# Attention kernel: TensorE's order from a search over 128 partial plans, and four sets of softmax weights instead of three

## The chip, the cores and the metric

The program runs on one core of a Trainium2 chip, in one launch. The metric is the device time of that launch in microseconds (us), the median of several runs. Five engines work side by side, each through its own list of instructions in order: TensorE (PE, with PEld for its weight loads), VectorE (DVE), ScalarE (ACT), GpSimd (POOL) and SyncE (SP), which issues the DMAs here. They are held together by semaphores.

## The reference, cut to what matters

One block: attention with a latent space per head, layer norm, a mixture of eight experts with top-2 routing, layer norm. x is (4, 2048, 256), there are 16 heads, and the latent width L is 32. The change is in the attention:

```
q_for_k = q_lat @ wqk_w.T + wqk_b
att = jnp.einsum('bhql,bhkl->bhqk', q_for_k, k_lat) * L ** (-0.5)
causal = jnp.tril(jnp.ones((T, T), dtype=bool))
att = jnp.where(causal[None, None], att, -jnp.inf)
att = jax.nn.softmax(att, axis=-1)
y_lat = jnp.einsum('bhqk,bhkl->bhql', att, v_lat)
```

## The kernel before, in words

The stages run one after the other: projections (`project_heads`), attention (`attend`), mixing and routing (`mix_and_route`), experts, final norm.

Attention is cut into 16 slots (batch by group of HG = 4 heads), each with NC = 4 chunks of CH = 512 queries, so 64 chunks. TensorE has four kinds of work there:

- A **unit** (`max_unit`, L855): one matmul of 128 queries against up to 512 keys, only to find each query's maximum. VectorE reads the bank and reduces it: L996 below the diagonal, L1000 with the causal edge added on it. 2560 units, four banks (MAXB).
- A **score** (`score`, L867): one matmul of 128 keys against up to 512 queries, with the negative maximum carried in two extra rows of q. ScalarE takes its exponential into `probs` (L941). 2560 scores, three banks (SCOREB). Four scores, one a head, make a key step.
- A **weigh** (`weigh`, L883): the four heads' weights of one key step times v, four matmuls into four groups of 32 partitions of one bank, `acc`. 640 weighs. In the trace each matmul has two records, so a full step is eight. They use the array in a narrow form (128 x 32), the others the whole array; the code calls this "tiled".
- A **turn** (`turn_sums`, L894): at the end of a chunk ScalarE copies `acc` (L931), TensorE transposes it, VectorE divides (L1027, L1031).

`probs` holds PROBS = 3 key steps: the exponentials of step k wait until weigh k - 3 is done. On the diagonal GpSimd masks the weights before the weigh (L980). The maxima of a chunk are combined, split and transposed on VectorE (L1006 to L1022) behind the chunk's last unit. SyncE then puts them into q's extra rows with eight small DMAs (L784, `put_shift`), and only then may the chunk's first score start. SyncE's list also holds the loads of q, k and v for later chunks (`load`) and the stores of y (`store_y`).

The order of these four kinds of work is fixed when the kernel is built, by the class `Order`. It plays the stage through with a clock of its own (`now`) and durations for each engine, and at each step takes the work with the lowest price. A weigh that follows a weigh is taken first up to BURST = 2; a first weigh is dearer when fewer than GATHER = 2 are ready. The lists that come out (`units_before_score`, `scores_before_weighing` and the like) set TensorE's order and, through the same lists, where ScalarE reads `acc`, where VectorE divides, and where SyncE puts rows and stores y. These engines' own work keeps its sequence.

Of the kernel before, what the change touches and what calls it, by code (L numbers as in the profile page):

```python
# [10 lines left out]

# [14 lines left out]
P = 128  # L26
# [3 lines left out]
HG = P // L  # L30
G = H // HG
CH = 512
NC = T // CH
TT = CH // P
# [487 lines left out]
BURST = 2  # L522
GATHER = 2
EVEN = 0.1
JOIN = 0.1
MAXB, SCOREB = 4, 3
PROBS = 3
# [4 lines left out]
def chunk_of(s, c):  # L532
    return s * NC + c
# [20 lines left out]

class Order:


    MODE, DRAIN = 0.112, 0.17

    def __init__(self):  # L560
        self.units_before_score = [0] * NS
        self.scores_before_weighing = [0] * NK
        self.units_before_weighing = [0] * NK
        self.scores_before_turn = [0] * CHUNKS
        self.units_before_turn = [0] * CHUNKS
        self.weighed_before_turn = [0] * CHUNKS
        self.now, self.tiled, self.burst = 0.0, False, 0
        self.u = self.h = self.w = self.turned = 0
        self.vector = self.scalar = self.pool = self.queue = 0.0
        self.reduced, self.exped, self.weighed = [0.0] * NU, [0.0] * NS, [0.0] * NK  # L570
        self.masked, self.read, self.divided = {}, {}, {}
        self.rows, self.parts_due = {}, []
        while self.h < NS or self.w < NK or self.turned < CHUNKS:
            self.step()

    def starts(self):

        free, tiled = self.now + self.MODE * self.tiled, self.now + self.MODE * (not self.tiled)
        at = {}
        u, h, w = self.u, self.h, self.w  # L580
        if u < NU and chunk_of(*MU[u][:2]) - chunk_of(*KS[min(h, NS - 1) // HG][:2]) <= QBUF - 2:
            at["unit"] = max(free, self.reduced[u - MAXB] if u >= MAXB else 0.0)
        if h < NS and h // HG - PROBS < w:
            s, c, kt = KS[h // HG]
            first = h % HG == 0 and kt == 0
            if not first or chunk_of(s, c) in self.rows:
                at["score"] = max(free, self.exped[h - SCOREB] if h >= SCOREB else 0.0,
                                  self.rows[chunk_of(s, c)] if first else 0.0)
        if w < NK and HG * (w + 1) <= h:
            s, c, kt = KS[w]  # L590
            n = chunk_of(s, c)
            if kt or n == 0 or n - 1 in self.divided:
                at["weigh"] = max(tiled, self.exped[HG * w + HG - 1], self.masked.get(w, 0.0),
                                  self.divided[n - 1] if kt == 0 and n else 0.0)
        if self.turned in self.read:
            at["turn"] = max(free, self.read[self.turned])
        return at

    def step(self):
        at = self.starts()  # L600
        backlog = {"unit": max(self.vector - self.now, 0.0), "score": max(self.scalar - self.now, 0.0)}
        if self.tiled and "weigh" in at and self.burst < BURST and at["weigh"] - self.now <= JOIN:
            pick = "weigh"
        elif not self.tiled and "turn" in at and at["turn"] <= self.now + 0.05:
            pick = "turn"
        else:
            price = {}
            for kind, start in at.items():
                price[kind] = start - self.now
                if kind in backlog:  # L610
                    price[kind] += EVEN * backlog[kind]
# [9 lines left out]
        start = at[pick]  # L621
        if pick == "weigh":
            self.weigh(start)
        elif pick == "unit":
            self.unit(start)
        elif pick == "score":
            self.score(start)
        else:
            self.turn(start)

    def weigh(self, start):
        k = self.w
        self.scores_before_weighing[k], self.units_before_weighing[k] = self.h, self.u
        self.burst = self.burst + 1 if self.tiled else 1
        self.tiled = True
        self.now = start + (CH - first_query(k)) / 600 + 0.03
        self.weighed[k] = self.now + self.DRAIN
        n = chunk_of(*KS[k][:2])
        if k + 1 == LAST_STEP[n]:
            self.scalar = max(self.scalar, self.weighed[k]) + 0.49  # L640
            self.read[n] = self.scalar + 0.16
        self.w += 1
# [1367 lines left out]
```

## Time and profile before

| | us |
|---|---|
| median of 3 runs | 2953.5 (2951.43 to 2960.58) |
| the profiled execution | 2953.24 |
| its span | 2951.5 |

| engine | busy us | share of the span |
|---|---|---|
| PE | 2811.8 | 95% |
| PEld | 1915.6 | 65% |
| DVE | 2124.7 | 72% |
| ACT | 1828.5 | 62% |
| POOL | 803.5 | 27% |

The first unit of attention starts at 367.0 us and the last division ends near 2147, so attention takes 1780 of the 2951.5 us. A matmul's record includes the time in which its columns are still in the array, so records of neighbouring matmuls overlap, and "busy" hides short waits. The distance from one start to the next tells more.

### The profile page before, as it was taken

The numbers are of one execution on the slowest core, as the hardware profiler recorded it, in microseconds if no ns is written. First come the engines' busy times: TensorE is split into PE (matmuls) and PEld (weight loads), VectorE is DVE, ScalarE is ACT, GpSimd is POOL, SyncE is SP. The second block draws the span as 40 slices with busy tenths as digits, with TensorE's granted clock in tenths as the row PEclk, the third lists the DMA queues.
The fourth block names the chain that finished last, engine by engine and source line by source line (L and its number), as shares of the span: only waits on it lengthen the run. The fifth ranks groups of instructions, "written<-read, shape, count | busy, mean of one in ns | idle before, by whom it ended". The sixth has DMA issues, their size and how long they took to land. (4 is left out here: it accounts for less than half of the span.)

```text
span 2951.5 us, 48579 instructions
## 1 busy us (share of the span) xinstructions
PE 2811.8 (95%) x16538; PEld 1915.6 (65%) x16538; DVE 2124.7 (72%) x5590; ACT 1828.5 (62%) x3673; POOL 803.5 (27%) x785
## 2 busy tenths in 40 slices
PE   8999989999999999999999999999979996999991
PEld 7888755555555655555555555555457774899991
DVE  7888788888888888888888888888334443545444
ACT  5666535766666676666666676666745453655554
POOL 7888620110110110111111011011025554122332
PEclk9999978999999999999999999999989998999995
DMA  7787852413332432432431432331053320434326
GB/s 227 265 286 265 290 130 55 106 43 88 91 91 75 95 83 70 109 80 59 108 96 43 94 82 63 88 82 32 5 166 121 108 83 24 120 74 105 78 25 236
DMA packets 259529, 320.32 MB, mean 109 GB/s; under 512 B 70563, under 2 KB 157644, under 8 KB 258001
## 3 DMA queue, kind: packets, MB, share of 16 engines
q1 hardware_dynamic: 241616, 294.02, 35.3%
q0 software_dynamic: 17664, 23.19, 3.9%
q8 instruction: 132, 2.16, 0.3%
q14 instruction: 117, 0.95, 0.1%
HBM read 182.69 MB, written 143.95 MB: 111 GB/s over the span
## 5 line engine op out<-in xcount | busy, mean ns | idle before, releaser
L941 ACT ACTIVATE att_probs<-att_score_bank 128x512 f32<-128x512 f32 (+3 forms) x2560 | 1159.0, 549 | 590.2 <-PE att_score_bank L867 582.3
L996 DVE TENSOR_REDUCE att_partial_max<-att_max_bank 128x1 f32<-128x512 f32 x1536 | 1004.9, 687 | 119.1 <-PE att_max_bank L855 113.6
L855 PE MATMUL att_max_bank<-att_k_st,att_q_st 96*128 96x512 f32 (+3 forms) x1792 | 642.2, 382 | 7.9 <-DVE att_partial_max L996 6.8
L867 PE MATMUL att_score_bank<-att_q_st,att_k_st 98*128 98x512 f32 (+3 forms) x1792 | 641.4, 384 | 2.4 <-ACT att_probs L941 2.3
L1000 DVE CUSTOM_DVE_ANT_0 att_edge_sum<-att_max_bank,first_edge 128x128 f32<-128x128 f32 (+3 forms) x1024 | 481.9, 483 | 150.9 <-PE att_max_bank L855 150.5
L883 PE MATMUL att_acc_bank<-att_probs,att_v_st 128*32 128x512 f32 (+3 forms) x5120 | 545.5, 539 | 1.4 <-POOL att_probs L980 0.9
L980 POOL TENSOR_SCALAR_AFFINE_SELECT att_probs<-att_probs 128x512 f32<-128x512 f32 x256 | 162.8, 636 | 1314.9 <-ACT att_probs L941 1314.9
L867 PEld LDWEIGHTS att_score_bank<-att_q_st,att_k_st 98*128 98x128 f32 x1792 | 334.2, 188 | 188.8 <-ACT att_probs L941 107.2
L855 PEld LDWEIGHTS att_max_bank<-att_k_st,att_q_st 96*128 96x128 f32 x1792 | 344.0, 193 | 149.3 <-DVE att_partial_max L996 74.7
L883 PEld LDWEIGHTS att_acc_bank<-att_probs,att_v_st 128*32 128x32 f32 x5120 | 132.1, 109 | 246.1 <-issue 135.8
L241 POOL TENSOR_TENSOR proj_op_low<-proj_turned,proj_op_high 128x512 fp32r<-128x512 f32 x192 | 244.2, 1295 | 47.0 <-ACT proj_op_high L401 44.8
L1733 ACT ACTIVATE exp_hid_high<-exp_hid_bank,exp_b 128x512 fp32r<-128x512 f32 x128 | 88.3, 690 | 160.8 <-PE exp_hid_bank L1680 150.8
L1647 POOL DMA_INDIRECT z_rows<-exp_eo,exp_row_ids x64 | 108.3, 1692 | 288.9 <-DVE exp_eo L1792 258.9
L855 PE MATMUL att_max_bank<-first_k,att_q_st 96*128 96x512 f32 (+3 forms) x432 | 177.4, 422 | 5.4 <-DMA att_v_st<-v_tokens 3.8
L1396 ACT ACTIVATE mix_hid<-mix_hid_bank,mix_rb 128x512 f32<-128x512 f32 x128 | 88.1, 688 | 148.6 <-PE mix_hid_bank L1308 148.6
L1244 POOL DMA_INDIRECT dispatched<-mix_x,mix_scatter_idx x128 | 126.0, 984 | 178.6 <-DVE mix_x L1508 143.0
L867 PE MATMUL att_score_bank<-att_q_st,first_k 98*128 98x512 f32 (+3 forms) x432 | 165.6, 419 | 0.0
L401 ACT ACTIVATE proj_op_high<-proj_turned 128x512 fp32r<-128x512 f32 x192 | 121.2, 632 | 68.9 <-DVE proj_turned L470 67.2
L1802 DVE TENSOR_TENSOR exp_hid_low<-exp_hid,exp_hid_high 128x512 fp32r<-128x512 f32 x128 | 88.6, 692 | 87.9 <-ACT exp_hid L1736 87.9
L1695 PE MATMUL exp_eo_bank<-exp_w_high,exp_hid_high 128*128 128x256 f32 x512 | 146.1, 285 | 0.0
L1695 PE MATMUL exp_eo_bank<-exp_w_high,exp_hid_low 128*128 128x256 f32 x512 | 144.9, 283 | 0.0
L1695 PE MATMUL exp_eo_bank<-exp_w_low,exp_hid_high 128*128 128x256 f32 x512 | 144.9, 283 | 0.0
(239 smaller groups left out, 4466.7 us busy)
## 6 DMA issues: line engine op xcount, KB each, us to landing
qk_parts<-proj_parts SPq DMA_DIRECT2D x64, 1024.0 KB, 5.3
att_k_st<-qk_parts SPq DMA_DIRECT2D x168, 256.0 KB, 6.0
att_q_st<-qk_parts SPq DMA_DIRECT2D x159, 256.0 KB, 4.1
v_tokens<-proj_v_tok SPq DMA_DIRECT2D x64, 256.0 KB, 4.6
att_v_st<-v_tokens SPq DMA_DIRECT2D x64, 256.0 KB, 6.9
exp_w<-in_ew SPq DMA_DIRECT2D x16, 1024.0 KB, 8.2
first_q<-qk_parts SPq DMA_DIRECT2D x33, 256.0 KB, 3.9
dispatched<-att_empty_rows SPq DMA_DIRECT2D x8, 1036.0 KB, 4.1
```

The costliest lines, as they stand in the source:

```text
L241: nc.gpsimd.tensor_tensor(op_low[:, c % OPS, i], turned[:, c % 2, i], op_high[:, c % OPS, i].bitcast(F32), ALU.subtract).then_inc(lows_don ...
L401: nc.scalar.activation(op_high[:, c % OPS, i], turned[:, c % 2, i], ACT.Copy).then_inc(highs_done, 1)
L855: nc.tensor.matmul(max_ps[u % MAXB][:, 0:width], q_tile(n)[0:3 * L, j, t * P:(t + 1) * P], k_tile(g, kb)[0:3 * L, j, 0:width], start=True, ...
L867: nc.tensor.matmul(score_ps[h % SCOREB][:, q0:CH], k_tile(g, kt // TT)[:, j, (kt % TT) * P:(kt % TT + 1) * P], q_tile(n)[:, j, q0:CH], sta ...
L883: last = nc.tensor.matmul(acc[j * L:(j + 1) * L, q0:CH], v_st[:, g % 2, kt // TT, kt % TT, j * L:(j + 1) * L], probs[:, k % PROBS, j, q0:C ...
L941: nc.scalar.activation(probs[:, k % PROBS, j, q0:CH], score_ps[(HG * k + j) % SCOREB][:, q0:CH], ACT.Exp).then_inc(exped, 1)
L980: nc.gpsimd.affine_select(out=block_probs, in_=block_probs, pattern=[[0, HG], [1, P]], compare_op=ALU.is_ge, fill=zero, base=0, channel_mu ...
L996: nc.vector.tensor_reduce(best, bank[:], AX.X, ALU.max).then_inc(unit_reduced, 1)
L1000: nc.vector.tensor_tensor_reduce(out=edge_sum[:, u % MAXB, 0:width], in0=bank[:, 0:width], in1=edge[:, CH - width:CH], scale=1.0, scalar=L ...
L1244: pool.indirect_dma_start(d["disp"], bass.IndirectOffsetOnAxis(ap=scatter_idx[:, c[1] % SUBS, kt:kt + 1], axis=0), x1[:, c[1] % ROUND, kt ...
L1647: pool.indirect_dma_start(d["z"], bass.IndirectOffsetOnAxis(ap=row_ids[:, q % RING, t:t + 1], axis=0), eo[:, q % 2, t, :], None, compute_o ...
L1695: last = nc.tensor.matmul(eo_ps[i][:, t, :], x[:, m, part], w[:, sub, m], start=(m == 0 and n == 0), stop=(m == MC - 1 and n == 2))
```

## The change

`PROBS` goes from 3 to 4. `Order` is rewritten. It keeps up to 128 partial plans; every round extends each of them by one unit, score, weigh or turn, keeps of those that have done the same amount of each kind the one that is due to end first, and goes on with the 128 that are due first. "Due" is the plan's clock plus the cost of the work that is left, plus 0.1 us for each weigh left. The durations are new. The limit of two weighs in a burst is gone. The functions of `attend` are unchanged, but for the slot count.

```diff
--- before.py
+++ after.py
 CHUNKS = SLOTS * NC
-BURST = 2
-GATHER = 2
-EVEN = 0.1
-JOIN = 0.1
 MAXB, SCOREB = 4, 3
-PROBS = 3
+PROBS = 4
 QBUF = 6
...
+MATMUL, TILED, INTO_TILES, OUT_OF_TILES, RELOAD, SIGNAL = 0.0218, 0.028, 0.082, 0.222, 0.115, 0.06
+DRAIN, ROWS_PUT, BURST_SHARE = 0.172, 7.0, 0.1
+MASKED_MAX = {P: 0.207, 2 * P: 0.341, 3 * P: 0.475, 4 * P: 0.607}
...
-        if self.tiled and "weigh" in at and self.burst < BURST and at["weigh"] - self.now <= JOIN:
-            pick = "weigh"
...
-                if kind == "weigh":
-                    k = self.w
-                    while k < NK and HG * (k + 1) <= self.h and self.exped[HG * k + HG - 1] <= self.now + 0.9 * (k - self.w) + 0.3:
-                        k += 1
-                    few = k - self.w < GATHER and self.w + GATHER < NK
-                    price[kind] += 0.5 * few + 0.3 * max(0.0, 1.1 - backlog["unit"]) + 0.3 * max(0.0, 1.0 - backlog["score"])
-                if kind == "turn":
-                    price[kind] -= 0.1
-            pick = min(price, key=price.get)
...
+    WIDTH, ALIKE = 128, 1
...
+    def unit(self, plan):
+        u = plan.u
+        start = max(plan.now + OUT_OF_TILES * plan.tiled, max(plan.reduced[0] + SIGNAL, plan.last) + RELOAD)
+        p = plan.copy()
+        p.kind, p.now, p.last, p.tiled, p.u = "unit", start + self.unit_cost[u], start, False, u + 1
+        drained = start + self.columns[u] / 2400 + DRAIN
+        if self.diagonal[u]:
+            vector = (drained + 0.192 if drained > p.vector else p.vector) + MASKED_MAX[self.columns[u]]
+        else:
+            vector = max(p.vector, drained + 0.038) + 0.598
+        p.reduced = p.reduced[1:] + (vector + 0.075,)
+        vector += self.vector_extra.get(u, 0.0)
+        if u in self.rows_after:
+            p.rows += ((self.rows_after[u], vector + ROWS_PUT),)
+        p.vector = vector
+        return p
+    def score(self, plan):
...
+        p = plan.copy()
+        p.kind, p.now, p.last, p.tiled, p.h = "score", start + self.score_cost[h], start, False, h + 1
+        n = self.queries[k]
+        drained = start + n / 2400 + DRAIN
+        slot_free = plan.weighed[k - plan.w]
+        p.scalar = max(drained + 0.06 if drained > p.scalar else p.scalar, slot_free) + n / 1185 + 0.046
+        exped = p.scalar + (0.1 if n > P else 0.16)
+        p.exped = p.exped[1:] + (exped,)
...
+    def weigh(self, plan):
...
+        start = max(plan.now + INTO_TILES * (not plan.tiled),
+                    max(free + SIGNAL, plan.last) + (0.05 if plan.tiled else RELOAD))
+        p = plan.copy()
+        p.kind, p.now, p.last, p.tiled, p.w = "weigh", start + self.weigh_cost[k], start, True, k + 1
+        p.ready, p.weighed = p.ready[1:], p.weighed[1:] + (p.now + DRAIN,)
...
+    def followers(self, plan):
+        u, h, w = plan.u, plan.h, plan.w
+        step = min(h, NS - 1) // HG
+        if u < NU and self.of_unit[u] - self.of_step[step] <= QBUF - 2:
+            yield self.unit(plan)
         if h < NS and h // HG - PROBS < w:
...
+            yield self.score(plan)
+        if w < NK and plan.ready:
+            yield self.weigh(plan)
+        if plan.read is not None:
+            yield self.turn(plan)
+
+    def search(self):
+
+        p = Plan()
+        p.now = p.last = p.vector = p.scalar = p.pool = 0.0
+        p.tiled, p.u, p.h, p.w, p.t = False, 0, 0, 0, 0
+        p.reduced, p.exped, p.weighed = (0.0,) * MAXB, (0.0,) * SCOREB, (0.0,) * PROBS
+        p.ready, p.rows, p.read, p.divided = (), (), None, (-1, 0.0)
+        p.before = p.kind = None
+        plans = [p]
+        for _ in range(NU + NS + NK + CHUNKS):
+            alike = {}
+            for plan in plans:
+                for p in self.followers(plan):
+                    if p is None:
+                        continue
+                    p.due = (p.now + self.units_left[p.u] + self.scores_left[p.h] + self.weighs_left[p.w]
+                             + BURST_SHARE * (NK - p.w) + OUT_OF_TILES * p.tiled + 0.5 * (CHUNKS - p.t))
+                    alike.setdefault((p.u, p.h, p.w, p.t, p.tiled), []).append(p)
+            plans = []
+            for group in alike.values():
+                group.sort(key=lambda p: p.due)
+                plans += group[:self.ALIKE]
+            plans.sort(key=lambda p: p.due)
+            plans = plans[:self.WIDTH]
+        self.note(plans[0])
```

The diff does not show the order itself. The engine is PE in all three places; line numbers are those of each kernel (unit L855 and L898, score L867 and L910, weigh L883 and L926). The number of matmuls and their shapes is the same in both kernels.

First place, the opening: behind the second and third weigh of the first chunk (32x384 and 32x256), where the next chunks' units stand. Before:

```order
L867 MATMUL att_score_bank<-first_q,first_k 128x128 x2
L855 MATMUL att_max_bank<-first_k,att_q_st 128x512
L883 MATMUL att_acc_bank<-att_probs,att_v_st 32x384 x4
L883 MATMUL att_acc_bank<-att_probs,att_v_st 32x256 x4
L855 MATMUL att_max_bank<-att_k_st,att_q_st 128x512
L855 MATMUL att_max_bank<-att_k_st,att_q_st 128x128
L855 MATMUL att_max_bank<-first_k,att_q_st 128x512
L855 MATMUL att_max_bank<-att_k_st,att_q_st 128x512
L855 MATMUL att_max_bank<-att_k_st,att_q_st 128x256
L855 MATMUL att_max_bank<-first_k,att_q_st 128x512
L855 MATMUL att_max_bank<-att_k_st,att_q_st 128x512
L855 MATMUL att_max_bank<-att_k_st,att_q_st 128x384
```

After:

```order
L926 MATMUL att_acc_bank<-att_probs,att_v_st 32x384 x4
L898 MATMUL att_max_bank<-att_k_st,att_q_st 128x128
L898 MATMUL att_max_bank<-first_k,att_q_st 128x512
L910 MATMUL att_score_bank<-first_q,first_k 128x256
L898 MATMUL att_max_bank<-att_k_st,att_q_st 128x512
L910 MATMUL att_score_bank<-first_q,first_k 128x128 x2
L898 MATMUL att_max_bank<-att_k_st,att_q_st 128x256
L910 MATMUL att_score_bank<-first_q,first_k 128x128
L898 MATMUL att_max_bank<-first_k,att_q_st 128x512
L926 MATMUL att_acc_bank<-att_probs,att_v_st 32x256 x4
L898 MATMUL att_max_bank<-att_k_st,att_q_st 128x512
L898 MATMUL att_max_bank<-att_k_st,att_q_st 128x384
```

A run of 18 units with nothing between them is broken up: two to three units, then a score of the first chunk, then units again. Before has four such runs, of 36, 18, 13 and 20 units; the run of 36 that opens the stage is the same in both, and after it no run in the new order is longer than 7.

Second place, the middle of the stage: a burst of weighs with the units and scores around it. Before (x8 is two steps of four matmuls):

```order
L855 MATMUL att_max_bank<-first_k,att_q_st 128x512
L867 MATMUL att_score_bank<-att_q_st,att_k_st 128x512
L855 MATMUL att_max_bank<-att_k_st,att_q_st 128x512
L867 MATMUL att_score_bank<-att_q_st,att_k_st 128x512
L883 MATMUL att_acc_bank<-att_probs,att_v_st 32x512 x8
L855 MATMUL att_max_bank<-first_k,att_q_st 128x512
L867 MATMUL att_score_bank<-att_q_st,att_k_st 128x512 x2
L855 MATMUL att_max_bank<-att_k_st,att_q_st 128x512
```

After, a burst of three (x12 is three steps of four matmuls):

```order
L898 MATMUL att_max_bank<-att_k_st,first_q 128x512
L910 MATMUL att_score_bank<-att_q_st,att_k_st 128x512
L926 MATMUL att_acc_bank<-att_probs,att_v_st 32x512 x12
L898 MATMUL att_max_bank<-att_k_st,first_q 128x512
L910 MATMUL att_score_bank<-att_q_st,att_k_st 128x512
L898 MATMUL att_max_bank<-att_k_st,first_q 128x128
L910 MATMUL att_score_bank<-att_q_st,att_k_st 128x512
L898 MATMUL att_max_bank<-att_k_st,first_q 128x512
```

What moved: the next key step's weigh is held back until three are together, and the units and scores follow the burst. Counted over the whole list, the old order has 351 bursts of weighs: 62 single and 289 double. The new one has 324: 121 single, 108 double, 77 of three and 18 of four.

Third place, the end, where no units are left. Before:

```order
L867 MATMUL att_score_bank<-att_q_st,att_k_st 128x512 x8
L883 MATMUL att_acc_bank<-att_probs,att_v_st 32x512 x8
L867 MATMUL att_score_bank<-att_q_st,att_k_st 128x512 x8
L883 MATMUL att_acc_bank<-att_probs,att_v_st 32x512 x8
L867 MATMUL att_score_bank<-att_q_st,att_k_st 128x512 x8
```

After:

```order
L910 MATMUL att_score_bank<-att_q_st,att_k_st 128x512 x3
L926 MATMUL att_acc_bank<-att_probs,att_v_st 32x512 x4
L910 MATMUL att_score_bank<-att_q_st,att_k_st 128x512 x4
L926 MATMUL att_acc_bank<-att_probs,att_v_st 32x512 x4
L910 MATMUL att_score_bank<-att_q_st,att_k_st 128x512 x4
L926 MATMUL att_acc_bank<-att_probs,att_v_st 32x512 x4
L910 MATMUL att_score_bank<-att_q_st,att_k_st 128x512 x4
L926 MATMUL att_acc_bank<-att_probs,att_v_st 32x512 x4
L910 MATMUL att_score_bank<-att_q_st,att_k_st 128x512 x4
```

Pairs of weighs after eight scores become single weighs after four. 22 weighs are left behind the last unit before, 21 after.

## Rows read from the trace of the kernel before

**Rows 1.** busy time by stage of attention (start:end, length, busy us and count by engine, clock, DMA)

```profile
core 0: us, PE busy (x) PEld busy (x) DVE busy (x) ACT busy (x) POOL busy (x), PEclk, DMA share, GB/s
367.00:509.00 142.00, 129.41 (x559) 77.49 (x559) 117.10 (x322) 56.35 (x121) 23.96 (x19) 0.75 0.43 97
509.00:2089.00 1580.00, 1578.47 (x9673) 926.75 (x9672) 1334.47 (x3638) 1092.51 (x2421) 192.79 (x295) 1.00 0.33 78
2089.00:2147.00 58.00, 53.02 (x267) 19.75 (x265) 3.56 (x12) 37.99 (x85) 6.15 (x10) 0.94 0.02 3
```

**Rows 2.** waits of TensorE's weight loads in attention (total us, times, longest)

```profile
PEld att_score_bank L867 <- ACT att_probs L941: 141.8, 550, 0.8
PEld att_acc_bank L883 <- issue: 135.8, 489, 0.7
...
PEld att_max_bank L855 <- DVE att_partial_max L996: 94.0, 147, 6.2
...
PEld att_max_bank L855 <- DVE att_partial_max L1000: 43.1, 77, 0.8
```

**Rows 3.** timeline of PE in mid attention (start us, us, engine, line, work)

```profile
1003.37 1.92 PE L883 MATMUL att_acc_bank<-att_probs,att_v_st 128*32 128x512 f32 x16
1005.23 0.50 PE L855 MATMUL att_max_bank<-att_k_st,att_q_st 96*128 96x512 f32 x1
1005.57 0.40 PE L867 MATMUL att_score_bank<-att_q_st,att_k_st 98*128 98x512 f32 x1
1005.80 0.40 PE L855 MATMUL att_max_bank<-att_k_st,att_q_st 96*128 96x512 f32 x1
...
1008.75 0.40 PE L867 MATMUL att_score_bank<-att_q_st,att_k_st 98*128 98x512 f32 x1
1009.09 1.92 PE L883 MATMUL att_acc_bank<-att_probs,att_v_st 128*32 128x512 f32 x16
...
1023.93 0.34 PE L867 MATMUL att_score_bank<-att_q_st,att_k_st 98*128 98x384 f32 x1
1024.11 0.43 PE L855 MATMUL att_max_bank<-first_k,first_q 96*128 96x128 f32 x2
...
1024.59 1.06 PE L883 MATMUL att_acc_bank<-att_probs,att_v_st 128*32 128x512 f32 x8
1025.58 0.38 PE L867 MATMUL att_score_bank<-att_q_st,att_k_st 98*128 98x256 f32 x1
```

**Rows 4.** timeline of ACT and DVE across the same burst [idle before, releaser]

```profile
1006.06 3.54 ACT L941 ACTIVATE att_probs<-att_score_bank 128x512 f32<-128x512 f32 x7 [2.19 <-PE att_score_bank L867]
...
1005.76 1.89 DVE L996 TENSOR_REDUCE att_partial_max<-att_max_bank 128x1 f32<-128x512 f32 x3 [0.66 <-PE att_max_bank L855]
```

**Rows 5.** timeline of PE and DVE in the opening, 20 units alone

```profile
481.89 0.90 PE L855 MATMUL att_max_bank<-att_k_st,att_q_st 96*128 96x384 f32 x4
...
485.36 0.28 DVE L1000 CUSTOM_DVE_ANT_0 att_edge_sum<-att_max_bank,first_edge 128x128 f32<-128x128 f32 x1
...
487.10 0.28 DVE L1000 CUSTOM_DVE_ANT_0 att_edge_sum<-att_max_bank,first_edge 128x128 f32<-128x128 f32 x1
...
490.71 1.48 PE L867 MATMUL att_score_bank<-att_q_st,first_k 98*128 98x512 f32 x3
```

**Rows 6.** timeline of PE near the end, scores and weighs only

```profile
2113.70 0.96 PE L867 MATMUL att_score_bank<-att_q_st,att_k_st 98*128 98x512 f32 x3
2114.94 2.45 PE L867 MATMUL att_score_bank<-att_q_st,att_k_st 98*128 98x512 f32 x5 [0.28 <-ACT att_probs L941]
2117.32 1.92 PE L883 MATMUL att_acc_bank<-att_probs,att_v_st 128*32 128x512 f32 x16
2119.18 0.96 PE L867 MATMUL att_score_bank<-att_q_st,att_k_st 98*128 98x512 f32 x3
```

**Rows 7.** DMA issues from 509 to 2089 us

```profile
att_v_st<-v_tokens SPq DMA_DIRECT2D x56, 256.0 KB, 6.8
...
att_q_st<-att_max_rows SPq DMA_DIRECT2D x384, 2.0 KB, 1.7
```

More of the change, by code:

```diff
@@ L576, in starts @@
[L576 to L582, printed above, removed]
-        if h < NS and h // HG - PROBS < w:
[L584 to L597, printed above, removed]
@@ L631, in weigh @@
[L631 to L642, printed above, removed]
@@ L644, in unit @@
-    def unit(self, start):
-        u, columns = self.u, unit_columns(self.u)
-        self.tiled = False
-        self.now = start + columns / 2400 + 0.02
-        ready = self.now + self.DRAIN + 0.02
-        wait = 0.13 if on_diagonal(u) and ready > self.vector else 0.0
-        self.vector = max(self.vector, ready) + wait + columns / 960 + 0.07
-        self.reduced[u] = self.vector + 0.135
-        n = chunk_of(*MU[u][:2])
-        if u + 1 == UNITS_THROUGH[n]:
-            self.vector += 0.2
-            self.parts_due = [(u + 1, 0.17), (u + 2, 0.27), (u + 3, 0.2)]
-        while self.parts_due and (u >= self.parts_due[0][0] or u + 1 == NU):
-            self.vector += self.parts_due.pop(0)[1]
-            if not self.parts_due:
-                self.queue = max(self.queue, self.vector + 0.1) + 5.0
-                self.rows[UNITS_THROUGH.index(u + 1) if u + 1 == NU else n - 1] = self.queue + 2.0
-        self.u += 1
@@ L678, in turn @@
-    def turn(self, start):
-        n = self.turned
-        self.scores_before_turn[n], self.units_before_turn[n], self.weighed_before_turn[n] = self.h, self.u, self.w
-        self.tiled = False
-        self.now = start + 0.5
-        self.vector = max(self.vector, self.now + self.DRAIN) + 0.68
-        self.divided[n] = self.vector + 0.13
-        self.turned += 1
+        self.of_unit = [chunk_of(*MU[u][:2]) for u in range(NU)]
+        self.of_step = [chunk_of(*KS[k][:2]) for k in range(NK)]
@@ new lines, in score @@
+    def score(self, plan):
+        h, k = plan.h, plan.h // HG
+        free = plan.exped[0]
+        if h % HG == 0 and KS[k][2] == 0:
+            rows = [at for n, at in plan.rows if n == self.of_step[k]]
+            if not rows:
+                return None
+            free = max(free, rows[0])
+        start = max(plan.now + OUT_OF_TILES * plan.tiled, max(free + SIGNAL, plan.last) + RELOAD)
+        p = plan.copy()
[6 more added lines that the diff above has]
+        p.exped = p.exped[1:] + (exped,)
+        if h % HG == HG - 1:
+            if KS[k][2] >= TT * KS[k][1]:
+                p.pool = max(p.pool, exped + 0.1) + 0.64
+                exped = p.pool + 0.05
+            p.ready += (exped,)
+        return p
@@ new lines, in weigh @@
+    def weigh(self, plan):
+        k = plan.w
+        n = self.of_step[k]
+        free = plan.ready[0]
+        if KS[k][2] == 0 and n:
+            if plan.divided[0] < n - 1:
+                return None
+            free = max(free, plan.divided[1])
+        start = max(plan.now + INTO_TILES * (not plan.tiled),
[3 more added lines that the diff above has]
+        p.ready, p.weighed = p.ready[1:], p.weighed[1:] + (p.now + DRAIN,)
+        if k + 1 == LAST_STEP[n]:
+            p.scalar = max(p.scalar, p.now + DRAIN + 0.04) + 0.49
+            p.read = p.scalar + 0.05
+        return p
@@ new lines, in note @@
+    def note(self, plan):
+        self.total = plan.now
+        kinds = []
+        while plan.before is not None:
+            kinds.append(plan.kind)
+            plan = plan.before
+        self.units_before_score, self.scores_before_weighing, self.units_before_weighing = [], [], []
+        self.scores_before_turn, self.units_before_turn, self.weighed_before_turn = [], [], []
+        u = h = w = 0
+        for kind in reversed(kinds):
+            if kind == "unit":
+                u += 1
+            elif kind == "score":
+                self.units_before_score.append(u)
+                h += 1
+            elif kind == "weigh":
+                self.scores_before_weighing.append(h)
+                self.units_before_weighing.append(u)
+                w += 1
+            else:
+                self.scores_before_turn.append(h)
+                self.units_before_turn.append(u)
+                self.weighed_before_turn.append(w)
```

84 lines of the change are left out of this document (35 added, 49 removed).

## The prediction

> **What bounds the kernel now.** I read the busy time by stage first. Attention has three parts [rows 1]: an opening from 367 to 509 us, in which TensorE's granted clock is 0.75 of full on average and VectorE is busy 117.10 of 142 us; a steady part of 1580 us at full clock; and an end of 58 us without units, at 0.94. In the steady part TensorE's matmul records fill 1578.47 us, VectorE's 1334.47 (84%), ScalarE's 1092.51 (69%). So TensorE is the engine that sets the pace, and the question is how much of its time is work. The records of neighbouring matmuls overlap, so the 1578.47 can't tell.
>
> The distances from start to start can [rows 3]. Score to unit, 512 wide: 1005.57 to 1005.80, 0.23 us. A 384-wide score takes 0.18 (1023.93 to 1024.11), so each 128 columns cost about 0.05, and a 128-wide one about 0.08. Of 2560 units and 2560 scores, 1536 each are full and 1024 each lie on the diagonal with four widths in equal number, mean (0.23 + 0.18 + 0.13 + 0.08) / 4 = 0.155. That is 3072 x 0.233 + 2048 x 0.155 = 716 + 317 = 1033 us. A double burst occupies 1003.37 to 1005.23 = 1.86 us, a single one 1024.59 to 1025.58 = 0.99; the difference, 0.87, is one step, and 0.12 is fixed per burst. 384 full steps and 256 on the diagonal (scaled by 320/512 columns: 0.54) are 334 + 139 = 473 us. Around a burst two more distances are too long: the last score before it, 1008.75 to 1009.09, is 0.34 instead of 0.23, and so is the first unit behind it, 1005.23 to 1005.57. So a burst costs 0.12 + 0.11 + 0.11 = 0.34 us beside its steps; the 351 bursts are 119 us. The half clock of the opening and the end costs at most 142 x 0.25 + 58 x 0.06 = 39 us.
>
> 1033 + 473 + 119 + 39 = 1664 of 1780 us. The remaining 116 us are the 64 turns (four short transposes each, about 0.4 us a turn as an estimate by the 128-wide spacing with its weight load: 26) and real waits, about 90. The waits of the weight loads [rows 2] name them: for ScalarE to free a score bank (141.8 us in 550 waits, 0.26 each), for VectorE to free a max bank (94.0 + 43.1 us in 224 waits). Most of each such wait lies under a running matmul, which is why they add up to more than 90. The loads that wait for "issue" before a weigh, 135.8 us, lie within the bursts and are no pool of their own.
>
> The reading of the first rows is where a rule bears. The Trainium skill, page "Perfetto Trace Analysis", section "Identifying the Most-Contended Engine", says that matmul busy time is no measure of the distance to the roofline and that weight-load busy time and useful flops are. By the matmul row (1578.47 of 1580) there would be nothing to gain in the steady part; by the weight loads (926.75, 59%) there is. My sum goes by the spacings, which side with the page.
>
> **The change part by part.** The matmuls and their shapes stay; only places move, and one more slot of weights exists. Durations are of the profiled execution (2953.24 us; median 2953.5).
>
> 1. Fewer bursts. 351 become 324: 27 x 0.34 = -9.2 us. Nothing hides this, TensorE being the bound. Lower end: were only the fixed 0.12 saved, -3.2. Upper end -9.2. I take -9.2, since all three distances stand at every burst that I looked at.
>
> 2. The opening. Before, runs of 18, 13 and 20 units stand alone. In the run of 20, TensorE needs 481.89 to 490.71 = 8.8 us [rows 5], for units whose own spacings are 20 x 0.155 = 3.1: 0.28 us idle per unit. VectorE sets this: four diagonal units come every 487.10 - 485.36 = 1.74 us, 0.43 each. 51 units x 0.28 = 14 us, less the four that find free banks in each of the three runs (12 x 0.28 = 3): 11. The new order has scores and weighs between them and no run over 7. What comes back: VectorE is 82% busy in the opening, and its work is the same, so it can't all be saved. Ends 0 and -14; I take -8.
>
> 3. The steady waits, some 60 of the 90 us (the rest is the opening, and an end in which ScalarE sets the pace). Four slots remove no wait that the trace shows: ScalarE's waits in the middle are for scores, not for a free slot. They only let a weigh be held back for a burst of three or four, so the effect is through the order. I counted with the spacings above how close each bank's next use follows. A score bank is free some 1.1 us after its score starts (0.40 of matmul record and about half a microsecond of exponential, seven in 3.54 us [rows 4]). Scores that come within 1.1 us of the third before them: 407 before, 337 after. Units within 1.5 us of the fourth before them: 407 and 549. One gets better by a sixth, the other worse by a third, but units that wait find VectorE only a little late. At half of the pool each: -5 and a few back. Ends: -15, if the search did place each unit where its bank is free, and above nothing by the rival below. I take -3.
>
> 4. The end. Before, a period of two steps is 2119.18 - 2113.70 = 5.48 us [rows 6], 2.74 a step; it has two stretches in which ScalarE holds the scores back. After, a step alone: 0.99 for the single burst, 2114.94 - 2113.70 = 1.24 for three scores and the wait, and 0.42 for the fourth (2117.32 - 2114.94 less four spacings of 0.49): 2.65. Sixteen such steps: -1.5. Ends 0 and -3.
>
> 5. SyncE's queue moves with the order. Rows of maxima land in 1.7 us, v in 6.8 [rows 7]. Units run ahead of scores by 98 to 126 in the new order against 80 to 86, so the rows of a chunk are put earlier relative to its first score, which helps, while a load is needed earlier relative to the weigh that frees its buffer. The limit of QBUF - 2 chunks is the same in both; between the freeing weigh and the first use lies at least one whole chunk, four steps of 2.7 us at the least, against seven issues and a landing of 6.8. I take nothing; if it fails it costs a few us in each of a few chunks.
>
> 6. Everything behind attention is untouched and starts earlier by what attention saves.
>
> Sum: -9.2 - 8 - 3 - 1.5 = -21.7, so 2953.24 - 21.7 = 2931.5; by the median 2932.
>
> **The rivals.**
> - **More of the waits goes than I allow.** Items 1 and 2 at their full size, 3 at -12: about -32, 2921. For it: the search compares whole futures, where the old order only saw the next step. Against: the count of close units goes up.
> - **Only the bursts count.** VectorE fixes the opening anyway, and the steady waits only change their place: -9 from item 1 and nothing else, 2944. For it: VectorE at 82% in the opening. Against: 0.28 us idle per unit in the runs, while scores and weighs were there to be done.
> - **Nothing changes.** A plan made of durations is off by jitter at each of 5824 places, and what the bursts save is lost in new waits: 2953. For it: every wait in [rows 2] is short, 0.26 us in the mean for a score bank. Against: spacings repeat to 0.01 us.
> - **VectorE becomes the bound (slower).** Across a double burst VectorE empties its four banks and idles 0.66 us, ScalarE 2.19 [rows 4]. One step more adds 0.87 to each. Idle time of VectorE forced by bursts: before 289 x 0.66 = 191 us; after 108 x 0.66 + 77 x 1.53 + 18 x 2.40 = 232, which is 41 more. Before, VectorE has 1580 - 1334 = 246 us idle, 191 forced by bursts and 55 for other reasons. If those 55 remain, the steady part takes 1334 + 232 + 55 = 1621, 41 us longer; less items 1, 2 and 4 that is +22 at the least, 2975. It decides once VectorE, idle during a long burst, can't be fed faster behind it than now. Against: behind a burst the new order gives units in twos and threes (204 runs of three or more against 45), TensorE issues a unit in 0.23 where VectorE needs 0.6, and 121 single bursts force no idle time at all.
>
> **How the numbers follow.** The forecast, -13 to -27, has 0.56; more than that, 0.12; only the bursts 0.15; nothing 0.09; VectorE as the bound 0.08. Smallest difference that can be told here is about 0.3%, 9 us. Faster by more than that: the first two, and half of "only the bursts" (its -9 is the border): 0.76. Within 0.3%: the other half, the case of nothing and a little of the slower one, 0.17. Slower 0.07. The range 2920 to 2956 leaves out most of the slower case and the tail of the best one; the forecast's own is 2926 to 2940.
>
> **What would show it.** In the trace after: attention ends near 2125 instead of 2147 with the projections' end unmoved; 324 bursts, each with 0.34 us around its steps, a step still 0.87; in the opening no stretch in which units follow each other at VectorE's pace behind the first 36; VectorE's busy time the same and its share of the steady part at 85 to 86%; ScalarE waiting for scores in fewer but longer pieces; a period of 2.65 us at the end. Waits of weight loads for ScalarE lower, for VectorE equal or a little higher. Wrong would be a VectorE busy under 83% of the steady part, waits for `loaded` or for the rows of maxima, or an opening that is slower because the granted clock stays at its lower level (1.2 GHz) for longer: it is 0.75 on average there now, and each 10 us more at that level cost up to 5.

## The result: 2909.06 us, 43 us faster, twice what was forecast

| | before | after |
|---|---|---|
| median | 2952.47 us (2950.78 to 2960.58, 4 runs) | 2909.06 us (2908.65 to 2911.18, 4 runs) |
| span of the profiled execution | 2951.5 | 2909.4 |

The ratio is 0.9849 (95% interval 0.983 to 0.9868). The forecast was 2932, the range ended at 2920. The sign was right; the gain forecast, 21.7 us, was half of the 43.4 measured.

Busy time by stage of attention in the kernel after (columns as in [rows 1]); attention ends at 2101.6 us instead of 2147, its last unit starts at 2046 instead of 2089:

```profile
367.00:509.00 142.00, 135.71 (x683) 80.62 (x683) 129.15 (x373) 71.13 (x151) 23.88 (x19) 0.90 0.44 98
509.00:2048.00 1539.00, 1537.99 (x9577) 924.75 (x9576) 1307.05 (x3586) 1092.48 (x2401) 193.48 (x297) 1.00 0.34 81
2048.00:2101.60 53.60, 43.98 (x239) 17.53 (x239) 2.84 (x11) 33.41 (x73) 4.84 (x8) 0.90 0.02 3
```

The first row is the surprise: in the same 142 us TensorE ran 683 matmuls instead of 559, VectorE 373 instructions instead of 322, and the granted clock is 0.90 instead of 0.75. In the steady part VectorE is busy 84.9% of the time, against 84.5% (1334.47 of 1580) in [rows 1].

To see where the time went I compared both traces at equal work. "Work" is what TensorE has started so far, each unit, score, weigh and turn counted with its duration undisturbed (widths over 2.4 GHz plus the fixed part seen in the spacings of [rows 3]; all of attention is 1552 us of it). The starts in the two traces then give, for the time up to 90 us of work (the opening), from there to 1500 us (steady) and to the end. Each entry is of one profiled execution and good to about 1 us:

| us | opening | steady | end | behind attention |
|---|---|---|---|---|
| before | 145.6 | 1558.1 | 75.1 | 805.7 |
| after | 123.4 | 1534.5 | 75.6 | 809.0 |
| difference | -22.2 | -23.7 | +0.6 | +3.3 |

The waits of TensorE's weight loads in the whole of attention, kernel after, against [rows 2]:

```profile
PEld att_score_bank L910 <- ACT att_probs L984: 129.3, 425, 0.8
PEld att_acc_bank L926 <- issue: 123.7, 441, 0.8
...
PEld att_max_bank L898 <- DVE att_partial_max L1039: 64.6, 168, 0.8
PEld att_max_bank L898 <- DVE att_partial_max L1043: 58.7, 124, 0.8
```

Waits for ScalarE fall from 550 to 425, but only by 12.5 us; those for VectorE rise in number, 224 to 292, and fall in time, 137.1 to 123.3. Together these fall by 26 us, attention by 45, and most of each wait lies under a running matmul, so where the time went can't be read from them.

A burst of three, timeline of TensorE in the kernel after, to be set beside [rows 3]:

```profile
1010.51 0.41 PE L910 MATMUL att_score_bank<-att_q_st,att_k_st 98*128 98x512 f32 x1
1010.89 2.78 PE L926 MATMUL att_acc_bank<-att_probs,att_v_st 128*32 128x512 f32 x24
1013.60 0.50 PE L910 MATMUL att_score_bank<-att_q_st,att_k_st 98*128 98x512 f32 x1
```

It occupies 2.71 us, three steps of 0.87 and 0.10. The end, to be set beside [rows 6], has a period of 2077.26 - 2074.64 = 2.62 us a step, against the 2.65 worked out:

```profile
2074.64 0.97 PE L910 MATMUL att_score_bank<-att_q_st,att_k_st 98*128 98x512 f32 x3
2075.83 0.50 PE L910 MATMUL att_score_bank<-att_q_st,att_k_st 98*128 98x512 f32 x1 [0.22 <-ACT att_probs L984]
2076.26 1.07 PE L926 MATMUL att_acc_bank<-att_probs,att_v_st 128*32 128x512 f32 x8
2077.26 0.96 PE L910 MATMUL att_score_bank<-att_q_st,att_k_st 98*128 98x512 f32 x3
```

### The profile page after: what moved, and what is told of

Its sections match the earlier page's. It is cut to its first block and busy times, and to the rows that moved or that the text cites. A ratio compares the mean times of both kernels' runs of the same rounds, so it can differ in the third digit from the quotient of the medians.

```text
span 2909.4 us, 48579 instructions
## 1 busy us (share of the span) xinstructions
PE 2768.6 (95%) x16538; PEld 1915.1 (66%) x16538; DVE 2111.3 (73%) x5590; ACT 1838.4 (63%) x3673; POOL 802.8 (28%) x785
## 5 line engine op out<-in xcount | busy, mean ns | idle before, releaser
L910 PE MATMUL att_score_bank<-att_q_st,att_k_st 98*128 98x512 f32 (+3 forms) x1792 | 602.6, 381 | 6.9 <-DMA att_q_st<-att_max_rows 4.3
L898 PE MATMUL att_max_bank<-att_k_st,att_q_st 96*128 96x512 f32 (+3 forms) x1792 | 602.6, 378 | 0.9 <-DVE att_partial_max L1043 0.3
L926 PE MATMUL att_acc_bank<-att_probs,att_v_st 128*32 128x512 f32 (+3 forms) x5120 | 536.7, 536 | 2.4 <-POOL att_probs L1023 1.0
L910 PEld LDWEIGHTS att_score_bank<-att_q_st,att_k_st 98*128 98x128 f32 x1792 | 331.0, 189 | 193.1 <-ACT att_probs L984 101.5
L898 PEld LDWEIGHTS att_max_bank<-att_k_st,att_q_st 96*128 96x128 f32 x1792 | 331.0, 190 | 137.1 <-DVE att_partial_max L1039 44.7
L926 PEld LDWEIGHTS att_acc_bank<-att_probs,att_v_st 128*32 128x32 f32 x5120 | 134.9, 109 | 233.6 <-issue 123.7
L898 PE MATMUL att_max_bank<-first_k,att_q_st 96*128 96x512 f32 (+3 forms) x432 | 175.3, 419 | 4.8 <-DMA att_v_st<-v_tokens 4.3
L910 PE MATMUL att_score_bank<-att_q_st,first_k 98*128 98x512 f32 (+3 forms) x432 | 153.1, 401 | 0.0
```

What stands on the lines that cost most here:

```text
L898: nc.tensor.matmul(max_ps[u % MAXB][:, 0:width], q_tile(n)[0:3 * L, j, t * P:(t + 1) * P], k_tile(g, kb)[0:3 * L, j, 0:width], start=True, ...
L910: nc.tensor.matmul(score_ps[h % SCOREB][:, q0:CH], k_tile(g, kt // TT)[:, j, (kt % TT) * P:(kt % TT + 1) * P], q_tile(n)[:, j, q0:CH], sta ...
L926: last = nc.tensor.matmul(acc[j * L:(j + 1) * L, q0:CH], v_st[:, g % 2, kt // TT, kt % TT, j * L:(j + 1) * L], probs[:, k % PROBS, j, q0:C ...
```

## What the opening hides

The rows of the opening that I had not read before the prediction, from the trace of the kernel before (VectorE, GpSimd, TensorE, SyncE, TensorE):

```profile
399.58 6.44 DVE L1011 CAST att_max_parts<-att_neg_max 128x16 fp32r<-128x16 f32 x1
...
399.07 6.92 POOL L972 MEMSET att_k_st<- 2x8192 f32 x1
...
406.10 0.58 PE L855 MATMUL att_max_bank<-att_k_st,att_q_st 96*128 96x256 f32 x1 [5.88 <-DVE att_partial_max L996]
...
406.67 4.94 SPq L784 DMA_DIRECT2D att_q_st<-att_max_rows  x8
...
413.69 1.48 PE L867 MATMUL att_score_bank<-att_q_st,first_k 98*128 98x512 f32 x3
```

The CAST copies 128 x 16 elements; its median over 64 chunks is 0.165 us. Here it takes 6.44, because it starts half a microsecond after GpSimd's MEMSET and ends when that ends. VectorE stands, TensorE finds no bank for 5.88 us, and the rows of maxima of chunk 1 are issued only at 406.67, so that chunk's first score starts at 413.69. The Trainium skill, "GPSIMD Engine Reference", section "Specifications", says that GpSimd shares its SBUF interfaces with VectorE, with contention for VectorE's instructions in a two-port mode or with two SBUF inputs. The CAST has one SBUF input, so by that page it would have to run in a two-port mode, which no trace here shows. What the pair does show is the price: the whole of what is left of the MEMSET.

The same place in the kernel after: the chunk's last unit comes earlier, so the CAST is over before the MEMSET starts. The order also puts the rows ahead of the load of chunk 4 in SyncE's list (score 11 instead of 16, the load stands at score 12):

```profile
397.29 0.16 DVE L1054 CAST att_max_parts<-att_neg_max 128x16 fp32r<-128x16 f32 x1
...
401.94 6.92 POOL L1015 MEMSET att_k_st<- 2x8192 f32 x1
...
398.54 5.84 SPq L827 DMA_DIRECT2D att_q_st<-att_max_rows  x8
...
406.79 1.05 PE L910 MATMUL att_score_bank<-att_q_st,first_k 98*128 98x512 f32 x2
```

The first score of chunk 1 starts at 406.79 instead of 413.69: 6.9 us, from two meetings that the order moved and no part of the change aimed at. Across this MEMSET (401.94 to 408.86) VectorE's reductions of banks keep their usual 0.68 us, so the MEMSET does not stop all of VectorE's work.

## The experiments

Each is timed against the kernel before on the same chip, whose medians there were 2954.62, 2953.75 and 2953.32 us in the three groups of four runs. "Opening" and "steady" are the times between the same points of work as above, from the profiled execution.

**Which stretch carries the gain.** Two hybrids. The first plays TensorE's first 400 pieces in the old order and lets the search go on from there; the second is the reverse.

```diff
+OPENING = kinds_of(OldOrder())[:400]
+        for kind in OPENING:
+            p = getattr(self, kind)(p)
         plans = [p]
```

> The kernel after, but TensorE's first 400 pieces of attention stand in the old order (with its runs of 18, 13 and 20 units alone); from there on the search orders the rest, with four slots. Theory A (the opening is worth 22 us of the 43, of it about 14 by the granted clock): 2909 + 22 = 2931, with the clock at its lower level for some 70 us until 509 us as before, and the steady part as fast as in the kernel after. Rival B (the opening's gain is by chance of the clock and goes with any order; the rest is what counts): 2909 to 2915.

> The kernel before, but TensorE's first 400 pieces of attention stand in the new order; from there on the old rule orders the rest, which keeps to three sets of weights. Theory A: 2953 - 22 = 2931, granted clock full from about 419 us on. Rival B (the steady part carries the gain): 2945 to 2953. If both this and the kernel with the old opening come to about 2931, the two parts add up.

Measured: 2932.0 us (2930.85 to 2932.76), ratio 0.9923 (0.9909 to 0.9937), and 2931.1 (2927.69 to 2932.24), ratio 0.9917 (0.9903 to 0.993). Opening and steady against before: -1.9 and -23.4 in the first, -19.1 and -2.2 in the second. The two halves add up (22.6 and 23.5 us against 43.4 together), each is worth some 22 us, and neither needs the other. In the first the CAST took 6.36 us again.

**The steady part: bursts or waits.** The price of a burst was measured in the kernel before, by putting the unit behind a double burst between its two weighs:

```diff
+        if kinds[i] == kinds[i + 1] == "weigh" and kinds[i + 2] == "unit":
+            kinds[i + 1], kinds[i + 2] = kinds[i + 2], kinds[i + 1]
```

> The kernel before, in which in each double burst that is followed by a unit that unit stands between the two weighs: 542 bursts instead of 351, nothing else moved. Theory A (0.34 us for each burst at every place): 191 x 0.34 = 65 us slower, 3018. Rival B (TensorE often waits for a bank anyway behind a burst, so that a switch hides part of it): 20 to 45 us slower, 2973 to 2998.

Measured: 3013.29 us (3012.73 to 3020.17), ratio 1.02 (1.0185 to 1.0216). 59.5 us for 191 bursts is 0.312 us each. The 0.34 of [rows 3] was nearly right on average over these places, and little of it is hidden when the rest of the order stays.

Then the search with at most two weighs in a row:

```diff
-        if w < NK and plan.ready:
+        twice = plan.kind == "weigh" and plan.before.kind == "weigh"
+        if w < NK and plan.ready and not twice:
```

> The kernel after, but its search may put at most two weighs in a row: 382 bursts instead of 324. Theory A (my item 1: what the search gains in the steady part comes through fewer bursts, 0.34 us each): 58 x 0.34 = 20 slower than after, 2929. Rival B (the search gains by placing units and scores where their banks are free, and longer bursts are only one way to it): 2 to 8 slower, 2911 to 2917.

Measured: 2911.93 us (2909.53 to 2914.0), ratio 0.9854 (0.9839 to 0.9869). Theory A falls: 58 more bursts cost about 3 us, and the two intervals against the kernel before overlap. This order has 31 bursts more than the kernel before, and nearly the whole gain is there, so the gain does not depend on fewer bursts. With the price of a burst and the count in the steady part, what is left beside work and bursts is (steady time - 1410 us of work - bursts x 0.312):

| kernel | steady | bursts there | x 0.312 | waits |
|---|---|---|---|---|
| before | 1558.1 | 319 | 99.5 | 48.6 |
| after | 1534.5 | 278 | 86.7 | 37.7 |
| bursts of two | 1538.0 | 334 | 104.2 | 23.8 |
| three slots | 1545.0 | 318 | 99.2 | 35.7 |
| old durations | 1544.1 | 323 | 100.8 | 33.3 |
| 8 plans | 1552.8 | 317 | 98.9 | 43.9 |

Longer bursts and shorter waits are bought with each other: short bursts leave 14 us less of waits than the kernel after, and cost 17 us more in switches. The starts in the traces agree. In the steady part the distances around and within the bursts exceed the work by 0.31, 0.30 and 0.30 us a burst (before, after, bursts of two), and all other distances together exceed it by 48, 40 and 26 us. The search made the sum of the two smaller, not each of them.

**The slot, the durations, the width.** The edits are `PROBS = 3`; the old rule's constants in the new class (`INTO_TILES, OUT_OF_TILES, RELOAD, SIGNAL = 0.112, 0.112, 0.0, 0.0` and its formulas for banks and exponentials); `WIDTH = 8`. In all three a unit also waits in the plan until the load of its chunk stands ahead in SyncE's list:

```diff
-        if u < NU and self.of_unit[u] - self.of_step[step] <= QBUF - 2:
+        if u < NU and self.of_unit[u] - self.of_step[step] <= QBUF - 2 and h > self.load_at[self.of_unit[u]] + 8:
```

The kernel after has no such hold, and no run has the hold alone, so each difference to the kernel after below is of two edits.

> The search with three slots of softmax weights, as the kernel before has, and four slots nowhere; a unit is also held until SyncE's list has passed the load of its chunk. 359 bursts. Theory A (the slot serves the bursts: 35 more bursts at 0.34): 12 slower than after, 2921. Rival B (the fourth slot is what frees ScalarE, and the search alone brings little): 2935 to 2950. Rival C (the slot does nothing): 2909.

> The kernel after (search over 128 plans, four slots), but the search plays with the old rule's durations: 0.112 us for a switch either way, nothing for a weight load behind a wait, banks free later than in the trace, exponentials by n/1400 + 0.12. Units are also held until SyncE's list has passed their load. Theory A (looking ahead is what gains, the durations matter little): 2909 to 2916. Rival B (a search is only as good as its durations: the steady part's gain goes mostly): 2922 to 2940.

> The kernel after with 8 partial plans in place of 128 (units also held until SyncE's list has passed their load): 365 bursts, and three more runs of 13 to 14 lone units in the opening. Theory A (how far the search looks is what the steady part gains from; with few plans it is no better than the old rule): 2930 to 2940. Rival B (the durations do it, any look ahead is enough): 2910 to 2918.

Measured: three slots 2924.98 us (2920.15 to 2925.38), ratio 0.9894 (0.9879 to 0.9909); old durations 2931.12 (2927.13 to 2933.22), 0.9925 (0.9911 to 0.9939); 8 plans 2943.84 (2940.89 to 2944.97), 0.9968 (0.9956 to 0.9981). Three slots give 13.1 of the steady 23.7 us, so the fourth slot (with the hold) is worth about 10 there and 16 in all. That lies between A and B of that run: 40 more bursts in the steady part account for 12.5 us, and the waits are 2 us shorter. The old durations fall within their Rival B: 14.0 us of gain in the steady part and a weaker opening, in which the profile has a clock of 0.87 and 12.6 us of gain instead of 22.2. With 8 plans three runs of 13 to 14 lone units are back, the opening gains 2.9 and the steady part 5.3; the time lies above both of its ranges. (The profiled execution of the old durations was 4 us below its median, so its two parts are rather too large.) Against before, the gain is 30 us without the fourth slot, 23 without the new durations and 9 with 8 plans, instead of 43: of these three edits, each with the hold, the width weighs most and the slot least.

**The opening: rows, collision, clock.** First the MEMSET in pieces, in the kernel before:

```diff
-                    nc.gpsimd.memset(k_st[3 * L:3 * L + 2, NC - 1:].bitcast(F32), 1.0).then_inc(ones_set, 1)
+                    for at in range(NC - 1, 2 * NC - 1):
+                        for j in range(HG):
+                            last = nc.gpsimd.memset(k_st[3 * L:3 * L + 2, at, j].bitcast(F32), 1.0)
+                    last.then_inc(ones_set, 1)
```

> The kernel before, its order untouched; only GpSimd's fill of the ones rows in the second half of k_st (one MEMSET of 6.92 us at 399 us, across which VectorE's CAST of the maxima took 6.44 us instead of 0.16) is done in 16 pieces. Theory A (some 6 of the opening's 22 us are this collision, which the new order missed by chance, and the stop of TensorE also cost clock): the CAST waits for one piece at most, 2953 becomes 2941 to 2948. Rival B (VectorE was free to wait there, TensorE had its banks full): 2951 to 2954.

Measured: 2954.94 us (2951.99 to 2961.5), ratio 1.0003 (0.9994 to 1.0012): nothing. The profile says why; CAST, the rows' DMAs with their times to landing, and the first score of chunk 1:

```profile
396.60 0.39 DVE L1014 CAST att_max_parts<-att_neg_max 128x16 fp32r<-128x16 f32 x1
...
397.80 5.43 SPq L784 DMA_DIRECT2D att_q_st<-att_max_rows  x8
...
DMA to landing us min/median/max: 8.4/9.9/11.3
...
411.23 1.62 PE L867 MATMUL att_score_bank<-att_q_st,first_k 98*128 98x512 f32 x3 [6.21 <-issue]
```

The collision is gone (0.39), the rows leave at 397.80, and then 2 KB take 8.4 to 11.3 us, since the loads of three chunks were issued ahead of them. TensorE stands for 6.21 us instead of 5.88; the row names no releaser, but the last of the eight DMAs is issued at 402.6 and lands 8.4 us or more later, just before the score starts. So in the next run that load went behind the rows:

```diff
-                if load_next < CHUNKS and h == HG * FIRST_STEP[chunk_of(g - 1, 0)] + 12 + 24 * c:
+                if load_next < CHUNKS and h == HG * FIRST_STEP[chunk_of(g - 1, 0)] + 12 + 24 * c + 12 * (load_next == NC):
```

> The kernel before, order of TensorE untouched, with the ones rows in 16 pieces (no collision with VectorE's CAST) and SyncE's load of chunk 4 put behind the rows of maxima of chunk 1 instead of ahead of them. With the pieces alone the eight small DMAs landed after 8.4 to 11.3 us, behind three loads, instead of 1.7 to 3.6. Theory A (two covers lie on the same wait, and the new order lifted both; together 6 us, and some clock): the chunk's first score at 405 to 407 us instead of 413.7, and 2942 to 2948. Rival B (TensorE gains nothing there, since VectorE sets the opening): 2951 to 2955.

Measured: 2945.49 us (2941.75 to 2951.53), ratio 0.9972 (0.9962 to 0.9982), 7.8 us. Its profile:

```profile
397.76 5.85 SPq L784 DMA_DIRECT2D att_q_st<-att_max_rows  x8
...
DMA to landing us min/median/max: 1.7/3.1/4.2
...
404.79 1.62 PE L867 MATMUL att_score_bank<-att_q_st,first_k 98*128 98x512 f32 x3
```

Two covers did lie on one wait, and lifting one showed nothing; moving the load alone was not run. The granted clock of 367 to 509 us is 0.81 here, against 0.75, so some of the 7.8 us may come with it. Then the clock itself. In two runs TensorE is given more to do where VectorE sets the pace, with units computed twice into the same bank (`u in RUNS` are the 51 lone units of the runs of 18, 13 and 20). The second has the two edits of the run before as well:

```diff
+                if u in RUNS:
+                    nc.tensor.matmul(max_ps[u % MAXB][:, 0:width], q_tile(n)[0:3 * L, j, t * P:(t + 1) * P],
+                                     k_tile(g, kb)[0:3 * L, j, 0:width], start=True, stop=True)
```

> The kernel before, in which each of the 51 units of the three runs that stand alone (18, 13 and 20 units) is multiplied twice into the same bank; VectorE sets the pace of these runs, so the second matmul fills TensorE's idle time. Theory A (of the opening's 22 us about 14 are the granted clock, which falls behind runs in which TensorE idles): the clock stays at its upper level behind the runs and the time falls by 5 to 12 us, 2941 to 2948. Rival B (the clock is given by something else, or the doubled matmuls cost what they bring): 2952 to 2960.

> The kernel of the run with the rows ahead of the load and the ones in pieces, and in it the 51 lone units multiplied twice (which alone gave 9.5 us by the clock). If the opening's 22 us are the chunk's late first score (6) plus the clock (9.5) and the rest is the runs of lone units themselves (6), this comes to 2936 to 2940. Rival: both work through the clock alone and do not add up, 2943 to 2946.

> The kernel after, in which each of the first 36 units, alone in a run at VectorE's pace, is multiplied twice. Theory A (the clock's first low stretch, 374 to 402 us, follows TensorE's idle time there): the clock comes up sooner, 2903 to 2907. Rival B (VectorE sets the pace in that stretch whatever the clock, and at half clock two matmuls take longer than VectorE's reduction): 2908 to 2916.

Measured: the first 2944.2 us (2941.55 to 2945.0), ratio 0.9965 (0.9951 to 0.9978); the second 2941.09 (2938.6 to 2943.49), 0.9958 (0.9945 to 0.9972); the third (`u < 36` in the kernel after) 2909.46 (2907.53 to 2911.25), 0.9851 (0.9836 to 0.9866). Stretch 367 to 509 us of, in this order, the first, the second and the third (columns as in [rows 1]):

```profile
367.00:509.00 142.00, 130.52 (x666) 79.25 (x664) 122.83 (x340) 60.86 (x134) 22.48 (x19) 0.90 0.44 97
```

```profile
367.00:509.00 142.00, 136.55 (x693) 80.96 (x692) 121.14 (x348) 64.92 (x140) 23.09 (x34) 0.90 0.42 97
```

```profile
367.00:509.00 142.00, 138.54 (x704) 85.12 (x703) 128.18 (x367) 68.70 (x147) 23.40 (x19) 0.89 0.44 98
```

More matmuls made the first kernel 9.5 us faster with the order unchanged. The collision is still in it (CAST 6.34 us, TensorE idle 4.53 us) and the chunk's first score starts at 411.80, so the gain is not that of the rows. The clock went from 0.75 to 0.90, the value of the kernel after: the lower level (1.2 GHz) followed stretches in which TensorE had little to do, in the runs of lone units. From 440 to 460 us it is 1.00 instead of 0.74, from 480 to 500 us 1.00 instead of 0.66. A small part of the 0.15 is not the edit's: from 377 to 395 us, ahead of the first doubled unit, it is 0.65 instead of 0.50, and other kernels with the old opening have 0.50 to 0.63 there. The second run adds only 3 to the first, less than the sum of 7.8 and 9.5, so it decides between neither of its two expectations: part of what the earlier rows give is clock as well. The third brings nothing on top of the kernel after. Its clock came up sooner (0.82 instead of 0.61 from 377 to 395 us) and was lower behind that (0.58 instead of 0.89 from 395 to 410), 0.89 on the whole. That VectorE sets the pace of the run of 36 whatever the clock is not shown by it.

## Why the prediction was half right

- **Item 1: the price of a burst held, its role did not.** 27 fewer at a measured 0.312 are -8.4 us; I had -9.2. But the order with 31 bursts more than before was as fast as the kernel after within 3 us: the search can pay the same sum in bursts or in waits.
- **Item 2, the lone runs, held about as far as it went.** From the kernel before with rows ahead, no collision and clock restored (2941) to the new opening with the old rule behind it (2931) are 10 us. Between them lie the order of units, scores and weighs and the 51 needless matmuls, whose own cost no run shows, so the order's share is about 10 us at most by this pair. I had -8. Its 0.28 us of idle time a unit set spacings at full clock against a stretch with a clock of 0.67 (482 to 491 us), so some of that was clock already.
- **What failed in item 2 is that I took nothing for the granted clock and for the chunk's first score.** I had read 0.75 in [rows 1] and charged 39 us of attention to it, but as a fixed cost. It falls where TensorE idles in the lone runs, and the change removes them: filling them with matmuls gave 9.5 us. The clock was named only as a danger. Together with the rows of chunk 1 (collision, and queue in SyncE's list) it is 12 us (2953.3 to 2941.1). Item 5 looked at SyncE's queue in the steady part alone and took nothing.
- **Item 3, the steady waits, was mis-sized.** -3 was taken; with the table above they fell from 48.6 to 37.7, -11. The bursts of the steady part fell by 41 and not by 27, -12.8, since 14 more stand in the opening and the end. Counting how many units come close behind the fourth before them said "a third worse" (407 to 549) and was no measure of waiting: VectorE waits went up in number and down in time. What counts is the sum over the pattern, not how many places are tight. The pool taken as 60 was 49.
- **Item 4**: the period was right (2.62), the end still took 0.6 more, with a clock of 0.90 there against 0.94 and 9 bursts more. **Item 6**: the stages behind took 3.3 us more. Their work is the same; the kernel after with its first 36 units doubled has the same stages and took 2.6 us less there, so most of this is what two profiled executions differ by.
- **The slower rival did not come.** VectorE idles longer behind a burst of three (the trace after shows 1.33 and 2.04 us before its next work; the rival had 1.53). Yet its idle time in the whole steady part is 232 us (1539 - 1307), which is what the rival reckoned for the bursts alone: the 55 us of other idle time did not stay beside them. The 204 runs of units against 45 were counted over the whole list; directly behind a burst stand 16 such runs in either order, so they were no reason. "Only the bursts" and "nothing" are excluded by the interval. The rival of a larger gain was summed too small: with item 2's own end of -14 and item 4 it comes to -36.7 and not -32, which lies outside the range stated; 43 lies beyond that too.
- **The rule on matmul busy time held.** The Trainium skill, page "Perfetto Trace Analysis", section "Identifying the Most-Contended Engine", calls matmul busy time no measure of the distance to the roofline. The trace agrees: the record share stayed at 99.9% (1537.99 of 1539) while the stretch lost 24 us; the weight loads' share went from 59% to 60%.

In sum: steady bursts -12.8, steady waits -11, clock and rows -12, the rest of the opening -10 (lone runs, net of 5 more bursts there), end and later stages +4 (with 9 more bursts, 2.8 us, in the end): -42, the difference of the two spans.

No experiment beats the kernel after; the two nearest are at 2909.46 and 2911.93.

## What to carry to other kernels

Compare two orders at equal work, not at equal time: one table said which stretch each microsecond came from, and the waits did not. A stretch at a lower granted clock is no fixed cost: ask what the engine did before it and whether the change fills that. Count the price of a part only together with what the order trades it for: 58 more bursts at 0.312 us each cost 3 us in all. A wait can have two covers; where lifting one brings nothing, read what is late next before dropping the theory.

## What the runs showed of the hardware

- A CAST of 128 x 16 on VectorE took 6.44 us across a GpSimd MEMSET of 6.92 us, and 0.16 without it. With the MEMSET in 16 pieces it took 0.39. Reductions of banks kept their 0.68 us across the same MEMSET.
- Eight DMAs of 2 KB landed in 8.4 to 11.3 us with three chunks of loads ahead of them, the last issued 3.4 us before, and in 1.7 to 4.2 us with two.
- 51 needless matmuls in an opening made the kernel 9.5 us faster, by the granted clock (0.75 to 0.90).
- One more change into the 32-column form of the array and out of it costs 0.312 us on average, over 191 added to an order otherwise unchanged.
